# Reordering the prologue of a graph kernel: first inputs ahead of the first adjacency, folds of weights moved back

## What is computed

```
x = x + relu(norm_adj(adj) @ (layernorm(x) @ W0.T + b0))    # graph convolution (L0 gnn)
x = x + layernorm(x) @ WF.T + bF                            # linear layer (L0 ffn)
x = x + gru_gate(conv17(layernorm(x)), exp(-dist) * adj @ msg, layernorm(x))   # L1 gnn
x = x + thirty_times(tanh/silu/layernorm/linear)(layernorm(x))                 # L1 ffn
```

## Time and profile before

| what | value |
|---|---|
| median of 3 runs | 1299.74 us (1299.24 to 1300.05) |
| the profiled execution: its own time | 1298.93 us |
| the profiled execution: its span | 1297.2 us |
| PE busy | 1259.5 us, 97% of the span |
| DVE busy | 1192.2 us, 92% |
| ACT busy | 1003.6 us, 77% |
| POOL busy | 961.8 us, 74% |

### The profile page before, as it was taken

The page is one execution under the profiler, slowest core; times in us unless marked ns, Lnnn a source line. Parts: engine busy times, 40 slices in busy tenths (PEclk is TensorE's granted clock), DMA queues, the critical chain, the costliest instruction groups (busy, mean ns, idle before and its releaser), DMA issues.

```text
span 1297.2 us, 29539 instructions
## 1 busy us (share of the span) xinstructions
PE 1259.5 (97%) x9309; PEld 1123.3 (87%) x9309; DVE 1192.2 (92%) x2807; ACT 1003.6 (77%) x1408; POOL 961.8 (74%) x783
## 2 busy tenths in 40 slices
PE   8899999999999999689999999999999999999998
PEld 7677777777777777489999999999999999999998
DVE  7888888888888876899999999999999999999997
ACT  2455555555555554689999999999999999999995
POOL 3455555545555554399999999999999999999995
PEclk9999999999999999889999999999999999999999
DMA  6111111111111000000000000000000000000004
GB/s 191 41 42 42 46 55 55 47 40 40 40 40 40 0 1 1 1 2 0 0 0 0 0 0 0 0 0 0 0 0 0 0 0 0 0 0 0 0 0 130
DMA packets 29792, 27.71 MB, mean 21 GB/s; under 512 B 3269, under 2 KB 21448, under 8 KB 29640
## 3 DMA queue, kind: packets, MB, share of 16 engines
q1 hardware_dynamic: 29768, 27.41, 6.8%
HBM read 23.21 MB, written 4.19 MB: 21 GB/s over the span
## 4 chain that ended last, share of the span: by engine, by line
PE 83%; DVE 11%; issue 3%; ACT 2%; DMA 0%; POOL 0%; SPq 0%; DVEq 0%; ACTq 0%; POOLq 0%
PE psum L843 33%; PE psum L857 16%; PE psum L839 7%; PE psum L614 4%; PE psum L616 4%; PE psum L615 4%; PE psum L785 4%; PE psum L636 3%; PE psum L631 3%; DVE emb_n L1332 2%; DVE xh_mem L1190 1%; PE psum L625 1%; ACT emb_f L961 1%; PE psum L645 1%; DVE upd L1295 1%
## 5 line engine op out<-in xcount | busy, mean ns | idle before, releaser
L479 POOL TENSOR_TENSOR f_rs<-f_var,half_neg 128x8 f32<-128x8 f32 x240 | 396.6, 1653 | 28.6 <-DVE f_var L1248 10.4
L915 ACT ACTIVATE g_ring<-u_ring 128x1024 f32<-128x1024 f32 x240 | 392.6, 1636 | 3.0 <-DVE u_ring L1239 3.0
L843 PEld LDWEIGHTS psum<-w_t,y_all 128*128 128x128 f32 x2880 | 382.7, 193 | 9.3
L843 PE MATMUL psum<-w_t,y_all 128*128 128x128 f32 x2880 | 388.6, 275 | 0.0
L939 ACT ACTIVATE y_all<-psum 128x1024 f32<-128x1024 f32 x240 | 382.6, 1594 | 7.1 <-PE psum L857 7.0
L924 ACT ACTIVATE t_ring<-psum 128x1024 f32<-128x1024 f32 x232 | 373.7, 1611 | 3.2 <-PE psum L843 3.2
L1223 DVE BATCH_NORM_STATS2 f_stat<-g_ring 128x6 f32<-128x256 f32 x960 | 341.0, 415 | 0.1
L483 POOL TENSOR_TENSOR h_ring<-g_ring,f_rs 128x640 f32<-128x640 f32 x240 | 303.0, 1262 | 18.8
L1239 DVE SCALAR_TENSOR_TENSOR u_ring<-t_ring,psum 128x1024 f32<-128x1024 f32 x232 | 278.4, 1200 | 0.0
L857 PE MATMUL psum<-ident,h_ring 128*128 128x128 f32 (+1 forms) x1920 | 251.5, 274 | 7.4 <-DVE h_ring L1210 7.4
L857 PEld LDWEIGHTS psum<-ident,h_ring 128*128 128x128 f32 (+1 forms) x1920 | 231.5, 154 | 8.0 <-issue 8.0
(11 more groups left out here) (192 smaller groups left out, 2138.4 us busy)
## 6 DMA issues: line engine op xcount, KB each, us to landing
work<-in_adj_dram SPq DMA_DIRECT2D x16, 1024.0 KB, 5.5
x_tok<-in_x_dram SPq DMA_DIRECT2D x16, 256.0 KB, 5.6
out_dram<-y_all SPq DMA_DIRECT2D x8, 512.0 KB, 3.2
work<-in_L_gnn_conv_w_dram SPq DMA_DIRECT2D x1, 1088.0 KB
work<-in_L_gnn_w_ih_dram SPq DMA_DIRECT2D x1, 384.0 KB
work<-in_L_gnn_w_hh_dram SPq DMA_DIRECT2D x1, 192.0 KB
work<-in_L_gnn_W_dram SPq DMA_DIRECT2D x1, 64.0 KB, 5.2
work<-in_L_ffn_weight_dram SPq DMA_DIRECT2D x1, 64.0 KB, 4.8
```

The lines of the kernel that those rows point to most:

```text
L479: pool.tensor_tensor(f_rs[:, j % 4, :], f_var[:, j % 2, :], half_neg[:, 0:GT], ALU.pow).then_inc(f_pow, 1)
L843: m = pe.matmul(y_ps[k % 2][:, h, C * t:C * t + C], y_all[:, GT * k + NT * h + t, :], w1_t[:] if t < biased else w1c_t[:], start=False, st ...
L915: act.activation(g_ring[j], u_ring[j % 2], ACT.Silu).then_inc(f_silu, 1)
```

## The change

SP loads graph 0's inputs first, on a semaphore of their own (`s_x0`), and its adjacency second. DVE, instead of folding the first weights right after the constants, waits for those inputs, takes their statistics, and then adds the missing 16 to `s_in[0]` itself; the degree of graph 0 comes after. The fold of the first weights now stands behind `xs` (where `fold()` stood), its turning by PE stands between the two halves of the first aggregation, and ACT's copy of the turned matrices stands before `xh_t` (L971). `fold()` goes behind `stats(0, 1)` in the same step, just ahead of `weights_low(0, 4)`; `spread_vectors()` on PE goes from behind the first token product to behind the second layer's product; `take_rows()` goes from ahead of L1355 to behind `stats(2)`. The first `keep_awake` has 16 products instead of 20.

```diff
@@ SP
-            load(0, 0)
+            sp.dma_start(x_tok[:, graph(0), :], x_dram[0]).then_inc(s_x0, 16)
+            sp.dma_start(adj_in[0], adj_dram[0]).then_inc(s_in[0], 16)
@@ PE, start
-            keep_awake(DIST_B, 20)
-            pe.wait_ge(s_folded0, 1)
-            for j in range(2):
-                m = pe.transpose(bank[CONV][:, C * j:C * j + C], nat[:, N_W0 + j, :], ident[:])
-            m.then_inc(s_wturn0, 1)
+            keep_awake(DIST_B, 16)
+
+            def turn_first():
+                pe.wait_ge(s_folded0, 1)
+                for j in range(2):
+                    m = pe.transpose(bank[CONV][:, C * j:C * j + C], nat[:, N_W0 + j, :], ident[:])
+                m.then_inc(s_wturn0, 1)
@@ PE, step
                     aggregate(q, 0, 2)
+                    if b is None:
+                        turn_first()
...
                     if b is None:
-                        spread_vectors()
+                        pe.wait_ge(s_wload, 16 * NWEIGHTS)
                         turn_weights(0, 4)
...
                     tokens(bank[TOK], xh_t, WF, s_ffn)
                     if b is None:
+                        spread_vectors()
                         turn_weights(4, FILLS)
@@ ACT
-            act.wait_ge(s_wturn0, 1)
-            act.activation(w_full[:, W0:W0 + 2, :], tiles(bank[CONV])[:, 0:2, :], ACT.Copy).then_inc(s_wfull, 1)
...
                 if l0:
+                    if b is None:
+                        act.wait_ge(s_wturn0, 1)
+                        act.activation(w_full[:, W0:W0 + 2, :], tiles(bank[CONV])[:, 0:2, :], ACT.Copy).then_inc(s_wfull, 1)
@@ DVE, start: the fold of the first weights becomes fold_first(), same four instructions
@@ DVE, step
                                              op0=ALU.add, op1=ALU.mult).then_inc(s_xs, 1)
                     if b is None:
-                        fold()
+                        fold_first()
+                if ends(d, 0):
+
+                    dve.wait_ge(s_x0, 16)
+                    stats(0, 0)
+                    dve.sem_inc(s_in[0], 16)
                 if d is not None and (b is not None or not l0):
                     degree(d, p)
-                    if b is None:
-                        stats(0, d)
...
                         stats(0, d)
+                        fold()
                         weights_low(0, 4)
-                        take_rows()
...
                     stats(2, c)
+                    if b is None:
+                        take_rows()
```

More of the change, by code:

```diff
@@ L195, in build @@
         s_first = sem("s_first")
+        s_x0 = sem("s_x0")
         s_small = sem("s_small")
@@ L1072, in _, with fold_first @@
             link(ins)
[L1075 to L1080, removed]
+            def fold_first():
+                dve.wait_ge(s_first, 16 * 4)
+                first = nat[:, N_W0:N_W0 + 2, :]
+                link(dve.tensor_reduce(bcol[:, T0:T0 + 2], first, AX_X, ALU.add))
+                link(dve.tensor_tensor(bcol[:, U0:U0 + 2], bcol[:, B0:B0 + 2], bcol[:, T0:T0 + 2], ALU.subtract))
+                link(dve.tensor_scalar(bcol[:, T0:T0 + 2], bcol[:, U0:U0 + 2], 1.0 / C, None, ALU.mult))
+                dve.tensor_tensor(first, first, spread(bcol[:, T0:T0 + 2], 2, C), ALU.add).then_inc(s_folded0, 1)
             def fold():
```

## The result

| | median | range | ratio to before |
|---|---|---|---|
| before, 16 runs | 1299.22 us | 1297.86 to 1300.88 | |
| changed, 16 runs | 1302.34 us | 1300.25 to 1306.90 | 1.0029 (1.0022 to 1.0036) |

The change makes the kernel slower by 0.29%, 3.8 us on 1299.22; the two medians are 3.1 apart and the two means 3.7. The prediction was + 3.7 us and a median of 1303.4, 1.1 above the measured one. The profiled execution of the changed kernel is its best one, 1300.25 us with a span of 1298.3, 1.1 more than the span of the earlier trace rows; the runs spread over 6.7 us, those of the kernel before over 3.0. Both facts need an explanation.

What follows compares the result with a forecast made beforehand. DVE was taken to bound the prologue from 22.27 on, with PE busy behind it. Early gain - 0.3, `fold()` + 3.2 and `take_rows()` + 0.8 gave + 3.7: 1299.74 to 1303.4 us, range 1302.0 to 1306.0.

Steps and rivals of the forecast that it cites:

- Degree of graph 0 near 7.4: Start of the prologue: graph 0's degree starts at 7.4, when its transfers are complete, instead of 9.71.
- The early gain stops at graph 1's landing: DVE after graph 0's aggregate: ready at 21.9, it waits for graph 1's inputs until 24.2; 2.3 of 2.7 lost.
- rival of graph 1 in time: Graph 1's inputs land before DVE asks, keeping 2.3 more: shift 1.4, 1301.1 us; decided at a landing of 23.1; chance 0.05.
- - 0.3: Start of graph 1's degree on DVE: what is left of the early gain, 24.2 instead of 24.52.
- Contention of POOL and `fold_first()`: Behind `xs`, POOL's two sums of weights may lengthen `fold_first()` by 0 to 2.6; 2.3 of slack covers it.
- `fold()` + 3.2: Behind `stats(0, 1)`, where DVE is the bound, `fold()` is paid in full: 3.2, bounds 2.9 to 4.5.
- `take_rows()` + 0.8: Behind `stats(2)`, late `take_rows()` makes PE start graph 1's adjacency 3.7 later where DVE shifts 2.9: 0.8 more.
- the wait of PE for DVE at 35.7: Sign of being right: PE, 0.2 ahead, waits for `take_rows()` until 35.7 before turning graph 1's adjacency.
- Sum: Whole kernel: - 0.3 + 3.2 + 0.8 = + 3.7 us, median 1303.4; chance 0.62.
- the clock: PE's clock falls in a 3.9 gap before 27.6 and stays low at 33.5: + 1.9, shift 5.6, 1305.3 us; chance 0.18.
- its sign: PE in the prologue: a granted clock of 0.5 near 33 would speak for the clock's case.
- The loss is not taken up later: Rival: PE's 2.46 idle between 40 and 70 gives back up to that much; shift 1.2 to 3.7, 1301.6 us; chance 0.10.

Runs made afterwards that it cites:

- the second profile of the changed kernel: Changed kernel run once more, unaltered, against the kernel before: ratio 1.0034, 1300.53 to 1307.96 us; its profile has a span of 1299.4.
- the version with earlier transfers: Changed kernel with graph 1's transfers ahead of the small vectors and POOL's sums held until `fold_first()` is over: ratio 1.0019, median 1300.45, lowest 1299.21 us.
- the first profile: Profiled execution among the changed kernel's first runs, with the whole change against the kernel before: 1300.25 us, span 1298.3.
- both gaps filled: Changed kernel with 17 instead of 8 keep-awake products ahead of L629 and 8 more ahead of `spread_vectors()`: ratio 1.0024, median 1301.77 us.
- the version with ACT's issues: Changed kernel's early part alone, POOL's sums held until `fold_first()` is over, 11 small vectors issued by ACT instead of SP: ratio 1.0024, median 1302.06 us.

## Why the prediction was right, point by point

**Degree of graph 0 near 7.4.** It came at 6.85, with no wait for a transfer: right, and a little better than the landing at 7.4 that the prediction took over from before.

**The early gain stops at graph 1's landing.** Right as a mechanism, shown by the wait of 1.73 in the second profile of the changed kernel and by the version with earlier transfers, which started the degree 1.8 earlier and got 1.0 of lowest time back. The size was off: the degree started at 23.11 and 23.55, not 24.2, and at 23.1 lay the border that the prediction had set for its rival of graph 1 in time. The cause is that SP issued graph 1's inputs at 17.3 and 17.5 instead of 18.2. The term "- 0.3" of the sum was - 1.4 in the first profile and - 1.0 in the second. I had taken SP's queue as fixed; a transfer of weights that took SP 1.06 to issue took 0.49, and smaller differences make up the rest.

**Contention of POOL and `fold_first()`.** The prediction bounded it by 0 and 2.6: it was 2.1 (3.34 instead of 1.28) in the first profile and 1.0 in the second. The two-input instruction L1089 took 1.49 and 1.43 instead of 0.43, and ended 0.3 after one of POOL's sums had ended each time. The rule of the Trainium skill, "SBUF — State Buffer", section "SBUF: two separate sides", agrees with that. The other 1.0 of the first profile fell on L1088, which reads one tensor: it started at 13.75, inside POOL's sum of 13.57 to 14.89, and took 1.17; in the second profile it started 0.04 before that sum and took 0.17. As predicted the contention is absorbed: the second profile lost 1.0 less and started the degree of graph 1 no earlier.

**`fold()` + 3.2.** It took 2.84 (27.16 to 30.00), just under the prediction's lower bound of 2.9: POOL worked beside it from 27.43 on and none of its instructions took longer for it.

**`take_rows()` + 0.8.** The step as named was wrong. Put back, it gives nothing; PE's own chain behind the late `fold()` ends at the same time, and the wait of PE for DVE at 35.7 that the prediction named as a sign did not come. The term itself is there: from the degree of graph 1 to PE's turn of the adjacency it is 34.19 - 23.11 = 11.08 against 7.52, 3.56 more, of which 2.84 are `fold()` and 0.7 the rest: `spread_vectors()` and the turn of the weights now stand one after the other behind it. No run separates `spread_vectors()` from `fold()`, whose rows it reads.

**Sum.** - 1.4 + 3.56 = + 2.15 at PE's turn of the adjacency in the profile, and + 2.6 by the lowest runs, where the forecast had + 3.7. What lies between that and the measured + 3.8 goes with the clock, the rival that I had kept apart.

**The clock.** It was no rival but a part of the answer, in some executions and not in others. The gap before L629 came as foreseen, 2.21 and 3.69 long. At 33, where the prediction looked for its sign, the granted clock was back at 1.00 in both profiles. In the first the low stretch was over at about 30, when `fold()` ended, and was hidden behind it. In the second it reached to about 32 and PE's turn of the adjacency started at 35.22 instead of 34.19, of which 0.44 are the later degree of graph 1 and some 0.6 the slower products. With both gaps filled the ratio went from 1.0034 to 1.0024, about 1.3 us (by the medians 0.3 to 0.6), but the intervals overlap, so the share of the clock is known only roughly. That the forecast hit the total is in part luck: it counted 0.3 of the early gain where 1.0 to 1.4 came, and 4.0 for the late folds where 3.56 came, and the clock, which it had left out of the likeliest case, made up for both.

**The loss is not taken up later.** Right for the graphs, after 2.15 at PE's turn: 1.8 us at the first and 1.7 at the last. The 0.6 that the last layer gave back in that profile is not explained.

## What to carry to other kernels

An order that serves one engine earlier is worth only what the next outside event lets through: look up when the next stage's data land before counting a gain. Work that fills another engine's wait is free where it stands; moved by a few instructions into a stretch where its engine never idles, it costs its full length. And when a change opens gaps on TensorE, compare the runs' spread and mean granted clock with those of the kernel before, not one profile: here the profile showed the best of 16 runs.

## What the runs showed of the hardware

- The same program took 1300.25 to 1307.96 us, and the time followed the mean granted clock (0.990 to 0.985). Where an idle of 1.1, 1.9 or 3.7 us stood directly ahead of the products of `spread_vectors()`, the clock fell behind it in every profile; filling the 1.1 and the 1.9 with 8 products brought the mean clock back, from 0.9893 to 0.9907 and from 0.9892 to 0.9910.
- The length of an idle does not decide alone. Ahead of the turn of graph 0's tokens 1.88 us were followed by 0.50 in one version and by 1.00 in another. Ahead of the next turn 1.52 us were followed by 0.50 in the kernel before, and 1.56 by 1.00 in the changed kernel.
- At the low clock (0.50) the eight products of one column took 2.98 instead of 1.63, nearly twice as long.
- A transfer of a few bytes released its waiter 1.6 us after its issue with the DMA engines nearly idle (10 GB/s from 17.28 to 18.90 in the kernel before), and 6.6 us after it with larger transfers on the way (307 GB/s from 13.5 to 15.0 in the version with ACT's issues).
- An instruction of DVE on 256 numbers that reads one tensor took 1.17 instead of 0.17 us when it started inside a sum of POOL, and 0.17 when it started 0.04 before one.
